# Softmax attention in a decoder layer: the causal mask of the score maxima is added by VectorE, in one instruction with the maximum, and no longer by a matmul of TensorE

## The reference, cut to what matters

```python
q, k, v = (to_heads(q), to_heads(k), to_heads(v))
mem_k = to_heads(ext_mem)
k = jnp.concatenate([mem_k, k], axis=2)
v = jnp.concatenate([mem_k, v], axis=2)
att = jnp.einsum('bhtd,bhsd->bhts', q, k) * (1.0 / np.sqrt(HEAD_DIM))
causal = jnp.tril(jnp.ones((T, T), dtype=bool))
full_mask = jnp.concatenate([jnp.ones((T, mem_len), dtype=bool), causal], axis=1)
att = jnp.where(full_mask[None, None], att, -jnp.inf)
att = jax.nn.softmax(att, axis=-1)
y = jnp.einsum('bhts,bhsd->bhtd', att, v)
```

## Time and profile before

| | |
|---|---|
| Median of 3 runs | 2283.32 us (2280.03 to 2288.05) |
| The profiled execution | 2282.77 us |
| Its span, first to last instruction | 2281.1 us |
| TensorE busy | 1903.9 us (83%) |
| VectorE busy | 1494.6 us (66%) |
| ScalarE busy | 911.4 us (40%) |
| Mean clock granted to TensorE | 0.917 of full speed |

### The profile page before, as it was taken

How to read it: one execution, slowest core, us unless ns; L and a number is a source line. 1 busy time by engine, 2 the same in 40 slices (tenths; PEclk the granted TensorE clock), 3 DMA queues, 4 the chain that set the end, 5 groups by cost and what they waited for, 6 DMA issues and landing times. The chain is left out here.

```text
span 2281.1 us, 41052 instructions
## 1 busy us (share of the span) xinstructions
PE 1903.9 (83%) x14336; PEld 1267.0 (56%) x14336; DVE 1494.6 (66%) x3231; ACT 911.4 (40%) x1398; POOL 280.4 (12%) x353
## 2 busy tenths in 40 slices
PE   7929899886488157998999999946679999999997
PEld 5617666665355023433444444314468888888886
DVE  7925444443598455876877888614298787777776
ACT  5605454443133004655655666641233223323322
POOL 2100000000232001111111111134240000000000
PEclk9959999998799557999999999978799999999999
DMA  6932322331588320221211221136610000000000
GB/s 182 212 102 86 99 99 93 103 99 71 147 230 202 96 85 12 74 67 49 79 62 61 74 67 50 37 110 216 188 51 29 5 24 29 28 1 28 20 10 10
DMA packets 172803, 187.44 MB, mean 82 GB/s; under 512 B 87617, under 2 KB 143825, under 8 KB 166481
## 3 DMA queue, kind: packets, MB, share of 16 engines
q1 hardware_dynamic: 157152, 171.12, 25.3%
q10 hardware_dynamic: 15472, 13.84, 2.4%
HBM read 114.33 MB, written 70.20 MB: 81 GB/s over the span
## 5 line engine op out<-in xcount | busy, mean ns | idle before, releaser
L1378 DVE TENSOR_REDUCE sa_piece_max<-sa_ps_m 128x1 f32<-128x512 f32 (+4 forms) x1024 | 486.3, 531 | 184.6 <-PE sa_ps_m L1220 124.0
L1335 ACT ACTIVATE sa_prob<-sa_ps_s 128x1024 f32<-128x1024 f32 (+3 forms) x480 | 374.9, 825 | 370.3 <-PE sa_ps_s L1247 216.1
L1215 PE MATMUL sa_ps_m<-sa_k,sa_q 96*128 96x358 bf16 (+7 forms) x1024 | 268.9, 304 | 5.2 <-DVE sa_piece_max L1378 2.2
L1715 DVE SCALAR_TENSOR_TENSOR mo_acc<-mo_ps_o,mo_keep,mo_acc 128x256 f32<-128x256 f32 x512 | 212.2, 476 | 71.7 <-PE mo_ps_o L149 71.6
L1581 ACT ACTIVATE mo_h_hi<-mo_h 128x512 fp32r<-128x512 f32 x144 | 91.0, 632 | 272.2 <-DVE mo_h L1697 272.2
L1354 POOL TENSOR_SCALAR_AFFINE_SELECT sa_prob<-sa_prob 128x256 f32<-128x256 f32 x256 | 102.5, 406 | 676.6 <-ACT sa_prob L1335 674.0
L1247 PE MATMUL sa_ps_s<-sa_q,sa_k 99*128 99x512 bf16 (+3 forms) x768 | 180.2, 330 | 2.1 <-ACT sa_prob L1335 2.0
L577 DVE TENSOR_TENSOR la_att<-la_ps_att,la_cap 128x512 f32<-128x512 f32 x128 | 88.5, 691 | 141.6 <-PE la_ps_att L492 141.6
L1213 PE MATMUL sa_ps_m<-sa_km,sa_q 96*128 96x154 bf16 x512 | 125.1, 246 | 66.8 <-DMA sa_vm<-mem 48.8
L1213 PEld LDWEIGHTS sa_ps_m<-sa_km,sa_q 96*128 96x128 bf16 x512 | 51.1, 100 | 224.1 <-issue 139.8
L537 ACT ACTIVATE la_phi_kT<-la_ps_kT 128x512 f32<-128x512 f32 x128 | 76.4, 597 | 246.2 <-PE la_ps_kT L473 246.2
(11 more groups left out here) (187 smaller groups left out, 3782.2 us busy)
## 6 DMA issues: line engine op xcount, KB each, us to landing
s_y<-la_y SPq DMA_DIRECT2D x16, 512.0 KB
s_x<-cl_xn SPq DMA_DIRECT2D x16, 512.0 KB, 6.2
s_y<-sa_y SPq DMA_DIRECT2D x16, 512.0 KB, 2.6
mw_raw<-experts SPq DMA_DIRECT2D x18, 384.0 KB, 3.5
s_q_parts<-pj_parts SPq DMA_DIRECT2D x16, 384.0 KB, 4.8
s_k_parts<-pj_parts SPq DMA_DIRECT2D x16, 384.0 KB, 2.6
la_q<-s_q_parts SPq DMA_DIRECT2D x16, 384.0 KB
la_k<-s_k_parts SPq DMA_DIRECT2D x16, 384.0 KB
```

The lines of the kernel that those rows point to most:

```text
L1215: last = nc.tensor.matmul(ps_m[:, s, a - lo:hi - lo], qs, k[g][0:STACK, j, a - MEM:hi - MEM], start=lo > 0, stop=True, skip_group_check=True)
L1335: nc.scalar.activation(dst, src, ACT.Exp, scale=HD ** -0.5).then_inc(expd[s], 1)
L1378: nc.vector.tensor_reduce(piece_max[:, j, t, n:n + 1], ps_m[:, s, 0:hi - lo], AX.X, ALU.max).then_inc(piece_done[s], 1)
L1715: last = nc.vector.scalar_tensor_tensor(acc[:, t], ps_o[:, s, t], keep[:, n * TB + t, i - 1:i], acc[:, t], ALU.mult, ALU.add)
```

## The change

The mask matmul and its operand `eye` go. `later` stays in fp32 as loaded, with 512 columns of zeros in front of it, so that one row range of it gives zeros for the keys before the diagonal block and the mask for the block. For the 640 masked pieces VectorE issues `tensor_tensor_reduce`: it adds that range to the piece in PSUM, writes the sum back there, and gives the maximum of it, starting from -3e38. The other 384 pieces keep `tensor_reduce`. At the start a memset of 128 x 512 replaces the two casts. VectorE's loop over the batches is written out.

```diff
@@ softmax_attention
-        eye = ph.sb("eye", [P, P], BF16)
-        later_f = ph.sb("later_f", [P, P])
-        later = ph.sb("later", [P, P], BF16)
+        later = ph.sb("later", [P, BANK + P])
@@ SP
-            for dst, name in ((ident, "ident"), (later_f, "later")):
-                sp.dma_start(dst[:, :], io[name]).then_inc(consts_in, 16)
+            sp.dma_start(ident[:, :], io["ident"]).then_inc(consts_in, 16)
+            sp.dma_start(later[:, BANK:BANK + P], io["later"]).then_inc(consts_in, 16)
@@ TensorE, piece
-                a, e = max(lo, MEM + t * P), hi
-                if a < e:
-                    first = MEM + t * P
-                    last = nc.tensor.matmul(ps_m[:, s, a - lo:e - lo], eye[:, :], later[:, a - first:e - first],
-                                            start=False, stop=True, skip_group_check=True)
                 last.then_inc(piece_ps, 1)
@@ VectorE
-                    nc.vector.tensor_copy(eye[:, :], ident[:, :])
-                    nc.vector.tensor_copy(later[:, :], later_f[:, :]).then_inc(cleared, 1)
+                    chain.link(nc.vector.memset(later[:, 0:BANK], 0.0))
+                    dve.sem_inc(cleared, 1)
@@ VectorE, reduce_pieces
                     s = PIECE_BANK[m][0]
+                    first = MEM + t * P
+                    if first < hi:
+                        nc.vector.tensor_tensor_reduce(ps_m[:, s, 0:hi - lo], ps_m[:, s, 0:hi - lo], later[:, BANK + lo - first:BANK + hi - first],
+                                                       1.0, -BIG, ALU.add, ALU.max, piece_max[:, j, t, n:n + 1]).then_inc(piece_done[s], 1)
+                        continue
                     nc.vector.tensor_reduce(piece_max[:, j, t, n:n + 1], ps_m[:, s, 0:hi - lo], AX.X, ALU.max).then_inc(piece_done[s], 1)
@@ VectorE, the order
-            with dve.Fori(0, B - 1) as b:
+            for b in range(B):
                 chain.restart()
                 for g in range(QUADS):
                     quad(b, g)
-            chain.restart()
-            for g in range(QUADS):
-                quad(B - 1, g)
```

## The result

The changed kernel takes 2262.3 us (median of 7 runs, 2255.6 to 2271.0), the one before 2286.3 us beside it. The ratio is 0.9902 (95% interval 0.9881 to 0.9922), some -22 us. The forecast was 2295 us, 2264 to 2340. Of all executions reported here two, of 3695 and 3784 us, were far slower than the others of their kernel, and no ratio counts them.

The account below looks back on a forecast made before the run. Neither TensorE nor VectorE alone was taken as the bound, since they hand three PSUM banks back and forth. TensorE -20, VectorE +32 and the rest 0 sum to +12 on the 2283.3 us median: 2295 us, range 2264 to 2340.

Parts of the forecast that it names:

- What bounds the kernel: Paired work, 870 to 1470 us: neither TensorE nor VectorE alone sets the pace; they hand three PSUM banks back and forth.
- TensorE's term: Mask matmuls removed from TensorE: 2.0 us a quad, 30 over 15 quads, two thirds of it coming back, -20 us.
- VectorE's term: Masked pieces on VectorE: 600 at 0.12 us more each, 72 us, of which 0.45 lies on the path, +32 us.
- The price of a pair: VectorE's extra time per masked piece: 0.06 us for the richer form plus 0.06 for handing over the maximum, 0.12.
- The share on the path: Part of VectorE's added work that lengthens the kernel: 0.45, from 95 of 212 us of waits being for VectorE.
- The rest: Piece order, banks, semaphores, the starting memset and VectorE's written-out loop: taken as nothing, 0 us.
- My aside: At a batch's end, about 1032 to 1036 us: if VectorE's loop end caused the stand, some -4 us twice.
- (C): Rival, masked pieces on VectorE: maximum from the same stream for 0 to 0.03 us more, 2256 to 2270 us; chance 0.24.
- (D): Rival: VectorE becomes the bound, masked pieces cost 0.25 us more, a quad lasts 43.5 us, 2330 to 2360; chance 0.11.
- (E): Rival: VectorE's masked pieces stream at half rate, 2.1 ns a column, +140 us, 2425 us; chance 0.05.
- (B): Rival, balance: masked pieces cost VectorE 0.05 to 0.08 us more, +12 to +19 against -20, 2276 to 2290; chance 0.27.
- The hidden start: First quad: some 33 us more VectorE work would be hidden behind DMA loads, scores beginning no later than 867 us.

Follow-up runs that it names:

- e3: Kernel before with VectorE's batch loop written out and TensorE's mask matmuls left out, nothing in their place: ratio 0.9887 to the kernel before.
- e1: Kernel before with only VectorE's loop over the batches written out, mask matmuls and plain reductions kept: 2272.8 us, ratio 0.9956.
- e4: Changed kernel with TensorE's mask matmuls kept as well, so the mask is added twice: ratio 0.9975 to the kernel before.

## Why the prediction was wrong, point by point

**What bounds the kernel.** Right: neither engine alone. Removing 2.0 us of TensorE brought 1.2 to 1.5 a quad, adding 5.2 of VectorE cost 1.4.

**TensorE's term, -20.** Right within its error: -16 (e3 against e1, and the changed kernel against e4), or 15 x 1.2 = 18 to 15 x 1.5 = 23 by the quads.

**VectorE's term, +32.** This is the first step that failed, in two factors. The price of a pair was put at 0.12 us, 0.06 for the richer form and 0.06 for the read; it was 0.02. The 0.06 for the form came from an operation that reads a scalar per partition, and this one carries constants: the wrong neighbour, though no run shows that the scalar is what costs it the 0.06. The 0.06 for the read came from small steps in a row, each behind the other; the read lies wholly beside the next piece. The share on the path was put at 0.45 from the waits, and measured 0.27 at the price that I had assumed. Either factor put right alone would have left 5 or 19; the term measured +4, and part of that isn't the price at all but the bank's later release, which I had not priced. The rule of the Trainium skill ("VectorE: DVE Perf Modes", Two Vector instructions with no wait between them) that an accumulator written out is a second instruction holds (640 read records of 0.15 us), and my reading of it, that the second instruction has to cost its engine time, doesn't.

**The rest, 0.** The second step that failed, and the larger surprise: VectorE's loop written out is -10 us. I had seen the loop go, put its end to 1032 us where all engines stand, and there it is TensorE's loop end. VectorE's lies at 984, one quad ahead, as its work does. The row was in the waits of before all the time:

```profile
DVE sa_piece_max L1378 <- issue: 5.4, 2, 2.8
```

My aside that VectorE's loop end, if it were the cause, would be worth some -4 us twice came out near the size, by luck: it was read from another engine's stand.

**The rivals.** (C) covered the time, 2256 to 2270, and was right that the pair is nearly free, but not in its sum: TensorE's gain less the pairs is -12, and the other 10 are the loop's. That its range held the result is luck in that part. (D)'s mechanism is real, with its price somewhat over-stated. (E) is out: from the starts in the timeline above, (0.62 - 0.10) / (512 - 26) = 1.07 ns a column for the pairs, against 1.05 for the reductions. Without the loop the change would have been 2272 us, between (B) and (C). Two upper ends were wrong as sums: with the -20 of TensorE (B)'s terms give 2275 to 2282, not 2290, and the forecast's 0.09 to 0.18 us give 2288 to 2312, not 2322.

**What would show it.** The hidden start held (866.05), and the clock stayed at 1.00 in the quiet quads. A quad took 37.9 us and not 39.6, VectorE was busy for 33.0 of it and not 36, and the successor of a 512 wide masked piece came after 0.62 us and not 0.72: by these signs it was (C), save for the second record, which (C) had excluded. From 870 to 1470 us VectorE waited less for pieces, 49.1 + 39.2 = 88 us where it was 117. TensorE's weight loads waited more for reductions, 118 us where it was 95, the sign of a gain that is eaten: a quarter to 0.4 of the 2.0 us was.

## What to carry to other kernels

Price an operation by the distance to its successor beside the closest neighbour in its operands, and ask of each extra record whether it lies beside the next or before it. Where a diff writes a loop out, look for each engine's own loop end, at the place where that engine stands in the pipeline, in the waits that no engine ends ("issue"); a stand of 2.7 us cost 2.5 us of the whole, and 4 where TensorE's clock fell behind it; one of 3 to 4 us on TensorE itself cost 8. Test the parts of a change apart: here the part that looked like a side effect brought nearly half, and the same edit on TensorE's loop another 16 us.

## What the runs showed of the hardware that was not expected

- A VectorE instruction with a 512 wide sum into PSUM and a maximum lets its successor start after 0.62 us, against 0.60 for a plain reduction; the accumulator read (0.14 us) starts together with the successor.
- The end of a hardware loop held VectorE for 2.7 us and, at another place, TensorE for 3.0 to 4.3 us (7.2 us in two waits in the changed kernel, 7.3 before); with the lower clock behind it these cost 4 and 8 us of the whole.
- A wait taken by VectorE's sequencer as a step of its own, in place of a wait carried by the instruction, made 40 pieces cost a quad 0.9 to 1.0 us with no change in busy time (38.8 to 38.9 against 37.8 to 37.9 us, VectorE busy for 33.0 in both).
